# Flamingo gated cross-attention and ternary feed-forward layer: loads of weights issued behind the landing of a slot's exchange, sums of weights later in the slot

## The reference

```python
x = x + tanh(g_xattn[0]) * xattn(layernorm(x), ctx_512, Wq, w_kc_q, w_kc_kv, W_qr, W_kr, Wo)
x = x + tanh(g_ffn[0]) * ffn(layernorm(x), w1, g1, w2, g2, w3, g3)

# xattn: x is (2, 512, 512), ctx (2, 1024, 128), 16 heads of 128
q_big  = einsum('bshk,hkq->bshq', (hidden @ Wq.T).reshape(b, s, 16, 128), w_kc_q)
kv     = kv_c * cos + rotate_half(kv_c) * sin
q_r    = einsum('bshq,hqr->bhsr', q_big, W_qr)        # r = 64
k_r    = einsum('bld,hdr->bhlr', kv, W_kr)
attn   = softmax(einsum('bhsr,bhlr->bhsl', q_r, k_r))
ctx_c  = einsum('bhsl,bld->bhsd', attn, kv)
out    = einsum('bhsd,hkd->bshk', ctx_c, w_kc_kv).reshape(b, s, 2048) @ Wo.T

# ffn: every linear layer quantises its weights (512 x 2048 each) and its input
s  = mean(abs(w));  wq = round(tanh(w / (s + 1e-8))) * arctanh(s)
y  = act_quant(rmsnorm(x, g)) @ wq.T
ffn = linear(silu(linear(x, w1, g1)) * linear(x, w2, g2), w3, g3)
```

## Time and profile before

| | |
|---|---|
| median of 3 runs | 653.92 us (652.92 to 654.09) |
| the profiled execution | 656.19 us, of which the span of the core is 654.4 us |
| granted TensorE clock | 1.00 over the whole span |
| busy: TensorE / its weight loads | 635.1 us (97%) / 394.0 us (60%) |
| busy: VectorE, ScalarE, GpSimd | 536.5 us (82%), 422.2 us (65%), 360.2 us (55%) |
| DMA | 112.79 MB, mean 172 GB/s; SyncE's queue 104.24 MB, 60.1% of the 16 engines' span |
| exchange DMAs | 496 of 128 KB, median 2.6 us from issue to landing |
| DMA issues of feed-forward weights | 37 on SyncE's queue (median 4.8 us), 11 on ScalarE's (4.4 us), 512 KB each |

### The profile page before, as it was taken

How to read it: one execution, slowest core, us unless ns; L and a number is a source line. 1 busy time by engine, 2 the same in 40 slices (tenths; PEclk the granted TensorE clock), 3 DMA queues, 4 the chain that set the end, 5 groups by cost and what they waited for, 6 DMA issues and landing times.

```text
span 654.4 us, 9986 instructions
## 1 busy us (share of the span) xinstructions
PE 635.1 (97%) x2968; PEld 394.0 (60%) x2968; DVE 536.5 (82%) x870; ACT 422.2 (65%) x693; POOL 360.2 (55%) x304
## 2 busy tenths in 40 slices
PE   8789999999999999999999999999999998999997
PEld 7555466766766676666666666566656554545553
DVE  4778787788878877887789978997899987998863
ACT  2564686477737764776567766776666633598875
POOL 4722376655545554565367854664457144686651
PEclk9999999999999999999999999999999999999999
DMA  8207976788589858984988798878689872000001
GB/s 283 87 6 188 274 196 164 206 223 240 151 227 241 219 131 239 251 224 106 251 222 221 201 242 224 222 195 231 169 221 251 198 177 81 1 1 33 17 35 48
DMA packets 45208, 112.79 MB, mean 172 GB/s; under 512 B 11888, under 2 KB 15088, under 8 KB 45040
## 3 DMA queue, kind: packets, MB, share of 16 engines
q1 hardware_dynamic: 42128, 104.24, 60.1%
q10 hardware_dynamic: 2976, 8.06, 4.0%
q0 software_dynamic: 64, 0.00, 0.0%
HBM read 45.16 MB, written 2.10 MB: 72 GB/s over the span
## 4 chain that ended last, share of the span: by engine, by line
PE 68%; DVE 10%; SPq 8%; ACT 4%; issue 4%; DMA 3%; POOL 1%; PEld 1%; POOLq 0%; ACTq 0%; DVEq 0%; PEldq 0%
PE ps_s L1443 11%; SPq L1132 8%; PE ps_b L1476 6%; PE ps_s L623 5%; PE ps_ctx L1476 5%; PE ps_b L1339 4%; PE ps_b L1394 4%; DMA G<-E 3%; PE ps_b L1341 3%; PE ps_b L1413 3%; PE ps_b L1340 3%; ACT E L1675 2%; PE ps_b L674 2%; DVE small L1858 2%; PE ps_ctx L1472 2%
## 5 line engine op out<-in xcount | busy, mean ns | idle before, releaser
L1675 ACT ACTIVATE E<-ps_s,small 128x1024 f32<-128x1024 f32 x128 | 142.5, 1116 | 143.4 <-DVE small L1858 110.5
L1241 POOL TENSOR_TENSOR G_lo<-G,g_hi 128x512 fp32r<-128x512 f32 x130 | 168.0, 1306 | 117.7 <-ACT g_hi L1619 117.7
L1858 DVE TENSOR_REDUCE small<-ps_s 128x1 f32<-128x1024 f32 x128 | 149.8, 1211 | 34.5 <-PE ps_s L1443 34.3
L1872 DVE STREAM_TRANSPOSE E<-E 128x1024 f32<-128x1024 f32 x124 | 152.0, 1230 | 0.1
L1199 POOL TENSOR_SCALAR E<-E,small 128x1024 f32<-128x1024 f32 x64 | 78.9, 1233 | 109.6 <-DVE small L1864 98.0
L1619 ACT ACTIVATE g_hi<-G 128x512 fp32r<-128x512 f32 x130 | 76.9, 631 | 3.5 <-DVE wq L1888 3.5
L1339 PE MATMUL ps_b<-b_hi,ctx_hi 128*128 128x512 f32 x128 | 66.8, 522 | 0.3 <-DVE ctx_lo L1818 0.3
L1476 PE MATMUL ps_b<-G,kv 128*128 128x512 f32 x126 | 63.7, 600 | 1.7 <-DMA G<-E 1.7
L1476 PE MATMUL ps_ctx<-G,kv 128*128 128x512 f32 x126 | 64.6, 607 | 0.1
L1443 PE MATMUL ps_s<-k_hi,q_hi 64*128 64x512 f32 x256 | 57.3, 444 | 3.8 <-ACT E L1675 2.6
L623 PE MATMUL ps_s<-wq,q12T 128*128 128x512 fp8e4 x256 | 59.8, 379 | 0.1
(11 more groups left out here) (203 smaller groups left out, 1211.7 us busy)
## 6 DMA issues: line engine op xcount, KB each, us to landing
G<-E SPq DMA_DIRECT2D x496, 128.0 KB, 2.6
w_stage<-in_wffn SPq DMA_DIRECT2D x37, 512.0 KB, 4.8
w_stage<-in_wffn ACTq DMA_DIRECT2D x11, 512.0 KB, 4.4
wo_s<-in_woT SPq DMA_DIRECT2D x8, 512.0 KB, 5.4
wq_s<-in_wq SPq DMA_DIRECT2D x7, 512.0 KB, 5.5
wkcq_s<-in_wkcqT SPq DMA_DIRECT2D x7, 384.0 KB, 3.4
out<-x_sb SPq DMA_DIRECT2D x8, 256.0 KB, 2.0
x_sb<-in_x SPq DMA_DIRECT2D x3, 512.0 KB, 6.3
```

Of the source, the lines that this page charges most:

```text
L1241: nc.gpsimd.tensor_tensor(g_tile(w % 2, i, G_lo), tile, high_part(i).bitcast(F32).rearrange("p (t i q) -> p t i q", t=ST, i=4), ALU.subtra ...
L1675: nc.scalar.activation(out, scores, ACT.Exp, bias=negmax[:, k:k + 1], accum_out=rowsum[:, k:k + 1]).then_inc(exp_done, 1)
L1858: nc.vector.tensor_reduce(negmax[:, k:k + 1], ps_s[:, t % 2, :], AX_X, ALU.max, negate=True).then_inc(max_done, 1)
L1872: nc.vector.transpose(e_tile(w % 2, t), e_tile(w % 2, t)).then_inc(blocks_turned, 1)
```

## The change

```diff
-SUM_STEPS, TANH_STEPS, ROUND_STEPS = (1, 4), (0, 4), (4, 6)
+SUM_STEPS, TANH_STEPS, ROUND_STEPS = (4, 5), (0, 4), (4, 6)
...
+        def landed(sp, p, w):
+
+            sp.wait_ge(exchanged[w % 2], 2 * EXCHANGE * p + EXCHANGE * (w // 2 + 1))
+            sp.sem_inc(sp_passed, 1)
+
...
                 if not (variant == "last" and w == 3):
                     exchange(sp, *unit_ahead(p, w, 1))
+                    if variant != "last":
+                        landed(sp, *unit_ahead(p, w, 1))
```

## The result

The changed kernel takes 657.64 us (median of 13 runs, 655.65 to 661.7), the kernel before, beside it, 654.09 us (median of 13, 652.92 to 655.65). The ratio is 1.0057, with a 95% interval of 1.0042 to 1.0072: slower by 3.7 us, where 2.0 us less were forecast. The runs also spread over 6.0 us instead of 2.7. The profiled execution took 657.13 us, its span 655.3 us, against 656.19 and 654.4 us before. Medians and counts of executions from here on leave out five (two of e5, one of e6, two of e8) that took 712 to 2235 us.

The account below looks back on a forecast made before the run. TensorE was taken as the bound, busy 97% of the span, its gaps ended by slot 0's late exchange landing. Gains of 2.0 us at no cost, taken from the 653.92 us median, gave 651.9 us; range 650.5 to 655.9 us.

Parts of the forecast that it names:

- Price of the wait: 0: SyncE's wait for each landing was to cost nothing; far bound 2 us in each of pairs 1 to 3.
- Covered by 0.1 us: Pair 1 slot 3: landing near 177.5 us, exponentials done at 179.7, scores of pair 2 slot 0 starting at 179.82 us.
- The queue works the backlog off at some 0.2 us for each us: Exchanges starting behind loads: latency was to fall during the exchange, as from 4.9 to 3.0 us in pair 0 slot 1.
- by the same sum: Pairs 2 and 3: slot 3's landing was to be no later than the exponential, slot 2's issue lasting 10.05 us.
- the slots have more room: Pairs 4 to 6: one 512 KB load on SyncE's queue instead of two, so the wait was to cost nothing.
- gain of 2.0 us: TensorE's gaps behind slot 0 were to shrink by 1.0 in pair 2, 0.7 in pair 5, 0.32 us in pair 6.
- I carry the 2.0 us over: The gain read from the profiled execution of 656.19 us was taken from the median of 653.92 us, giving 651.9 us.
- later loads slow the last landing: Slot 0's last exchange DMA: loads issued behind it were said to raise its latency, in pair 2 from 3.5 to 4.5 us.
- rival 1: Later loads take nothing from slot 0's exchange; landings, gaps and time stay at 653.9 us; chance 0.28.
- The sums at steps 4 and 5: Twenty-four sums of 1.1 us moved into ScalarE's idle time ahead of step 6's exponential; cost 0, bound 1.1 us.
- Rival 2: Slots 2 and 3: late landings delay SyncE's loads and next exchange, TensorE stands in pairs 1 to 3; 657.9 us; chance 0.17.
- landing later than 177.6 us: Trigger of Rival 2: slot 3's landing in pair 1, forecast at 177.5 us, with 2.2 us of exponentials due by 179.82.

Follow-up runs that it names:

- e5: The changed kernel with the wait for the landing in slot 3 of each pair alone: 655.5 us, ratio 1.0013 to the kernel before.
- e6: The changed kernel with the wait in slots 0, 1 and 2, not in slot 3: 655.7 us, ratio 1.0019 to the kernel before.
- e8: The changed kernel with the wait in all slots of pairs 4 to 6 only: 658.6 us, ratio 1.0063 to the kernel before.
- e13: The changed kernel with all its waits, feed-forward loads cut from 512 to 128 KB in pairs 1 to 3 alone: 656.89 us, ratio 1.003.
- e2: The changed kernel with its waits in all slots, but the sums left at steps 1 and 4: 658.09 us, ratio 1.006.
- e10: The changed kernel without the wait in slot 3 of pair 6: 656.92 us, ratio 1.0042 to the kernel before.
- e1: The changed kernel without any wait for a landing, only the sums moved to steps 4 and 5: 654.78 us, ratio 1.0001.
- e3: The changed kernel with the wait in slot 0 of each pair alone: 653.69 us, ratio 0.9984 to the kernel before.
- e9: The changed kernel with every wait put behind the loads of its slot, not ahead of them: 654.34 us, ratio 0.9993.
- e11: The changed kernel with its waits, each feed-forward load behind pair 0 cut from 512 to 128 KB: 653.42 us, ratio 0.9978.
- e12: The changed kernel without waits, each feed-forward load behind pair 0 cut from 512 to 128 KB: 653.29 us, ratio 0.9979.
- e4: The changed kernel with the wait in slots 1 and 2 of each pair alone: 655.92 us, ratio 1.0022.
- e7: The changed kernel with the wait in all slots of pairs 0 to 3 only: 657.18 us, ratio 1.0032.
- e15: A second measurement of the same kernel as e8: 658.79 us, ratio 1.0067 to the kernel before.

## Why the prediction was wrong, point by point

1. **"Price of the wait: 0" is the step that failed.** The walk through pair 1 had the times of SyncE nearly right: the exchange of slot 3 at 164.39 us against 164.7 forecast, the last landing of slot 2 at 158.83 + 2.94 = 161.8 against 162.9, that of slot 3 at 173.89 + 4.25 = 178.1 against 177.5. Two things were wrong. The slower landing was undersized, 3.1 us for the last DMA of slot 3 where 4.25 were measured, and pair 2, where slot 2's last one took 5.67, was not walked through at all. And the landing was held against the exponential of step 6 and through it the scores of the next slot at 179.82 us, which is not its nearest consumer. The nearer one, TensorE's first product on the landed G, stood in the description of the kernel, but its rows were not read: 162.36 and 177.53 us. By the forecast's own numbers slot 2 would have been 0.5 us late and slot 3 exactly in time. "Covered by 0.1 us" was zero room against the right row. At the largest loss (231 us) the difference decides: the two exponentials, released at 228.17 us, were done by 230.4, in time for scores due at 230.63 (231.17 before, less the lag), while the product was due at 226.93 and began at 228.13.
2. **"The queue works the backlog off at some 0.2 us for each us"** was taken from pair 0, where 1 MB lay ahead. It held in pair 1 slot 2 (5.5 to 2.9) and failed in pair 2 slot 2, where the same loads end at 5.7 us. Pairs 2 and 3 taken "by the same sum", without a walk of their own, and pairs 4 to 6 by "the slots have more room" passed over this; e8, with waits in pairs 4 to 6 alone, costs 4.1 us, and e13's profile has its losses there. The step also counted nothing for the held-back loads' own landing: 8.68 us in e2 and 9.17 in e10, each with about 1 us or more lost on TensorE; in the changed kernel's profile this cost nothing.
3. **The gain of 2.0 us was sized from one execution.** The profiled execution of the kernel before took 656.19 us, 2.1 us above the median of 654.09 measured later, and its gaps of 1.39 + 0.82 + 0.32 us can account for that: without any wait they are absent in the profile of e1. The largest is in none of the other fifteen profiles, the others come and go. "I carry the 2.0 us over" to the median took from the median what was never in it. The changed kernel's profile has none of the three, 2.7 us by the ladder, which is in part luck and not the wait; e3 shows what the wait in slot 0 is worth over many executions, 1.0 us.
4. **That later loads slow the last landing** rests on the earlier trace rows and is borne out only in part. With loads directly behind, the last two landings in slot 0 of pair 2 took 4.1 us (median) in the trace of before, and 2.3 in e1. The Trainium skill (DMA: Bandwidth & Descriptors, section "Queues, rings and completion order") states that each DMA engine consumes descriptors in ring order. By that rule loads behind an exchange on the same queue would take nothing from it; e1 agrees in this place, before does not. The sign named for rival 1, a last landing above 4 us in slot 0 with no load behind it, is in e2: the last exchange DMA of pair 5 slot 0, issued at 382.77 us, took 4.40 us, the first load behind it was issued at 387.58, and a gap of 0.83 us followed. Rival 1 was right to doubt the gain, and left out the cost.
5. **The sums at steps 4 and 5 cost 0**: right, 1.0001 in e1. The mark named for a failure, gaps at steps 2 or 4, did not show.
6. **Rival 2** named the mechanism, the place (SyncE's burst of loads directly ahead of the next exchange, slots 2 and 3) and a time of 657.9 us; 657.64 was measured. Its gaps were expected ahead of the scores of step 1; most came ahead of the first product. That its time was met is in part luck: it priced 3 us in pair 1 and 1.5 in each of pairs 2 and 3, the ladder has 0.8, 1.6 and nothing behind the exchanges issued there, and 1.3 us in pairs 4 to 7. Its trigger, "landing later than 177.6 us", was met at 178.1. It had 0.17, because its price rested on a latency kept at 4.9 us, and "backlogs shrink in every exchange" was held against it, a statement on the trace of before, in which no such backlog stood there. The range ended at 655.9 us, as only a third of this rival was taken in.

## What to carry to other kernels

Before transfers are held back to let one land, count what then stands directly ahead of the next transfer that something waits for, and read for each landing its room: the time from its last issue to its first consumer, whichever engine that is. Read the same for the transfers held back. A gap seen in one profiled execution is priced only once it is known that it isn't that execution's own; a profile that lies above the median of the runs is a warning. Where only one slot of several can afford the burst, as slot 0 here, hold back there alone: e3 is the fastest complete kernel of this study, 1.0 us (0.3 to 1.8) below the kernel before and, by the two ratios, 4.8 us below the changed one.

## What the runs showed of the hardware

- **Late landings can cost clock as well.** The mean granted clock of each execution was taken along with its time. In the 117 executions of the kernel before for which it stands beside the experiments, and in the 78 of e1, e3, e6, e9, e10, e11 and e12, it is never under 0.999. In the changed kernel it is 0.997 in 2 of 13 executions, and in e2, e4, e5, e7, e8, e13 and e15 0.995 to 0.997 in 16 of 73, and these are long ones: in e15 four between 658.79 and 662.53 us against three from 655.29 to 657.13; in e2 four between 659.69 and 662.96 us against a median of 656.2 for the other eight. A share of 0.003 of 655 us is 2.0 us. The one such profile (e13, 0.997) shows where: the three stretches from 520 to 526 us lack 2 x (0.12 + 0.50 + 0.23) = 1.7 us of full clock, behind the idle time at the handover to pair 7. e15's profile has 1.73 us of idle time at the same place and stays at 1.00, so the gap does not decide alone. By these numbers it is part of why e8 and e15 are so slow, and of the wider spread; the changed kernel's 660.55 and 661.39 us at 1.000 it does not explain.
- **The last DMAs of an exchange land in 2.3 to 4.8 us at the same place**: in slot 0 of pair 5 the last two took (median) 3.9 us before, 3.1 in e1, 2.3 in e4 and 4.8 in e5 with a load directly behind, and 4.2 in e2, 3.1 in e3 and 2.3 in e6 with none. What makes the difference is open.
- **The profiled execution was not typical**, in both directions: 2.1 us above the median for the kernel before, 3.5 us below it for e15. Where a change makes the spread grow, the ladder of one execution shows mechanisms and not their mean price.
